# Moving the products dt times x of units 2 to 15 from GpSimd to VectorE in a one-core language-model tower

## The reference, cut to what matters

```python
def step(h, inp):
    u_t, dt_t, B_t, C_t = inp
    dA = jnp.exp(dt_t[..., None] * A)
    h = h * dA + (dt_t * u_t)[..., None] * B_t[:, None, :]
    y = jnp.einsum('bdn,bn->bd', h, C_t)
    return (h, y)
...
dt = jax.nn.softplus(x_dbl[..., :R] @ dt_w.T + dt_b)
```

## Time and profile before

| | |
|---|---|
| median of three runs | 551.28 us |
| the profiled execution | 551.16 us |
| its span in the trace | 549.3 us, 5677 instructions |
| VectorE (DVE) busy | 483.8 us, 88% |
| GpSimd (POOL) busy | 478.5 us, 87% |
| TensorE (PE) busy | 465.3 us, 85% |
| ScalarE (ACT) busy | 373.3 us, 68% |

### The profile page before, as it was taken

One profiled execution on the slowest core, in us unless ns is written; L12 is line 12 of the kernel. 1 busy time (PEld: TensorE's weight loads), 2 busy tenths in 40 slices (PEclk: granted clock), 3 DMA queues, 4 the chain that ended last, 5 costly groups with the idle time before them and its releaser, 6 DMA issues.

```text
span 549.3 us, 5677 instructions
## 1 busy us (share of the span) xinstructions
PE 465.3 (85%) x1659; PEld 181.0 (33%) x1659; DVE 483.8 (88%) x602; ACT 373.3 (68%) x656; POOL 478.5 (87%) x153
## 2 busy tenths in 40 slices
PE   6896886979799797979898889888997887795987
PEld 2432322323233232424233424343333332332333
DVE  3679879779898999999999999998899999999951
ACT  2475877476867777786968687858776885374633
POOL 5773889978979989899999999999999999999810
PEclk9897999889979898989999989979899998796999
DMA  5468641765071724426172717181717171700000
GB/s 60 27 48 236 209 155 40 249 217 157 32 242 38 234 78 150 162 93 218 62 231 83 239 63 248 54 253 54 252 50 253 58 253 48 256 16 10 0 11 19
DMA packets 50256, 70.79 MB, mean 129 GB/s; under 512 B 15874, under 2 KB 16818, under 8 KB 50226
## 3 DMA queue, kind: packets, MB, share of 16 engines
q1 hardware_dynamic: 47954, 69.20, 38.5%
q0 software_dynamic: 1024, 1.05, 3.3%
q10 hardware_dynamic: 1248, 0.19, 0.2%
HBM read 58.36 MB, written 9.96 MB: 124 GB/s over the span
## 4 chain that ended last, share of the span: by engine, by line
PE 36%; DVE 32%; issue 15%; ACT 8%; POOL 8%; DMA 0%; DVEq 0%; ACTq 0%; POOLq 0%
DVE st L1600 16%; DVE st L1585 6%; PE ps L638 6%; POOL st L506 5%; PE ps L731 3%; PE ps L719 3%; POOL st L497 2%; ACT ps L1114 2%; PE ps L813 2%; PE ps L549 2%; PE ps L699 2%; PE ps L681 2%; PE ps L829 2%; PE ps L612 2%; PE ps L665 2%
## 5 line engine op out<-in xcount | busy, mean ns | idle before, releaser
L506 POOL TENSOR_TENSOR st<-st,repC 128x2048 f32<-128x2048 f32 x63 | 285.9, 4547 | 21.0 <-ACT carry L1120 13.6
L1600 DVE TENSOR_TENSOR_SCAN st<-ps,carry,st 128x512 f32<-128x512 f32 x192 | 235.2, 1267 | 10.9 <-ACT ps L1114 10.3
L1114 ACT ACTIVATE ps<-dtS,negA 128x512 f32<-128x512 f32 x256 | 170.9, 682 | 47.2 <-DVE st L1600 43.9
L497 POOL TENSOR_TENSOR st<-duS,repB 128x2048 f32<-128x2048 f32 x31 | 141.0, 4548 | 2.0 <-PE ps L719 2.0
L1600 DVE TENSOR_TENSOR_SCAN st<-ps,zero,st 128x512 f32<-128x512 f32 x64 | 78.9, 1269 | 5.8 <-ACT ps L1114 5.4
L719 PE MATMUL ps<-st,fold 128*32 128x512 f32 x504 | 70.4, 625 | 15.4 <-POOL st L506 15.4
L1585 DVE TENSOR_TENSOR st<-duS,ps 128x2048 f32<-128x2048 f32 x32 | 72.7, 2271 | 0.2 <-PE ps L699 0.2
L638 PE MATMUL ps<-act,wT 128*128 128x512 f32 x128 | 57.7, 593 | 0.0
L470 POOL DMA_INDIRECT x<-in_L_tok_ple_table,idx x32 | 31.2, 976 | 12.5 <-issue 9.1
L681 PE MATMUL ps<-xr,wT 128*32 128x512 f32 x32 | 19.6, 697 | 22.5 <-DVE st L1585 22.5
L813 PE MATMUL ps<-xfT,w 97*128 97x512 f32 x64 | 35.2, 642 | 1.3 <-ACT xfT L1139 0.7
(11 more groups left out here) (150 smaller groups left out, 633.1 us busy)
## 6 DMA issues: line engine op xcount, KB each, us to landing
repC<-bc_dram SPq DMA_DIRECT2D x64, 256.0 KB, 4.8
duS<-du_dram SPq DMA_DIRECT2D x60, 256.0 KB, 3.3
dtS<-dt_dram SPq DMA_DIRECT2D x60, 256.0 KB, 4.2
repB<-bc_dram SPq DMA_DIRECT2D x31, 256.0 KB, 3.0
dt_dram<-dt SPq DMA_DIRECT2D x15, 256.0 KB, 3.2
du_dram<-du SPq DMA_DIRECT2D x15, 256.0 KB, 2.0
bc_dram<-bc_sb SPq DMA_DIRECT2D x16, 64.0 KB, 4.7
dtS<-dt SPq DMA_DIRECT2D x4, 256.0 KB, 5.7
```

The lines of the kernel that those rows point to most:

```text
L497: pool.tensor_tensor(st[:, r], duS[:, u % 2], row, ALU.mult).then_inc(sem("dbu_pool"), 1)
L506: pool.tensor_tensor(st[:, r], st[:, r], row, ALU.mult).then_inc(sem("hc_ready"), 1)
L1114: sc.activation(decay_bank(u, r, q), dtS[:, u % 2, q], ACT.Exp, scale=negA[:, way(u), q, r:r + 1]).then_inc(sem("decay_ready"), 1)
L1600: dve.tensor_tensor_scan(st[:, r, q, order], decay_bank(u, r, q)[:, order], st[:, r, q, order], first, ALU.mult, ALU.add).then_inc(sem("sc ...
```

## The change

For units 2 to 15, VectorE multiplies dt by x, and takes dt from the PSUM bank `PRE`, where TensorE has summed it, and not from ScalarE's copy. It still waits for `dt_ready`, that is, for the copy to be done. In units 2 to 13 the product for unit u+2 stands in slot 8 of VectorE; in unit 1 the product for unit 2 stands in slot 3 and that for unit 3 in slot 12. GpSimd keeps the product of unit 1 alone (unit 0's was VectorE's already).

Since the bank `PRE` is read until the product is done, what overwrites it waits for `du_ready` too: `conv` in that bank, and `pre`. ScalarE's `dt_out` no longer waits for `du_ready`, except for unit 2 (the copy `dt` is no longer an input of the product).

```diff
@@ gpsimd @@
-            def dt_times_x(u):
-                pool.wait_ge(sem("dt_ready"), u + 1)
-                if u == 1:
-                    for q in range(NQ):
-                        pool.wait_ge(sem(f"du_first_{q}"), 16)
-                else:
-                    pool.wait_ge(sem("du_in_dram"), 16 * (u - 1))
-                pool.wait_ge(sem("x_ready"), u + 1)
-                pool.tensor_tensor(du[:], dt[:], x_of(u), ALU.mult).then_inc(sem("du_ready"), 1)
+            def second_du():
+                pool.wait_ge(sem("dt_ready"), 2)
+                for q in range(NQ):
+                    pool.wait_ge(sem(f"du_first_{q}"), 16)
+                pool.wait_ge(sem("x_ready"), 2)
+                pool.tensor_tensor(du[:], dt[:], x_of(1), ALU.mult).then_inc(sem("du_ready"), 1)
...
                 if u == 0:
-                    dt_times_x(1)
+                    second_du()
                 if 2 in on_pool(u):
                     input_product(u, 2)
-                if u == 1:
-                    dt_times_x(2)
                 by_c(u, 0)
                 by_c(u, 1)
                 if u + 1 < UNITS:
                     input_product(u + 1, 0)
                 by_c(u, 2)
-                if 0 < u < UNITS - 2:
-                    dt_times_x(u + 2)
@@ tensor @@
                 if bank == PRE:
                     pe.wait_ge(sem("dt_ready"), u)
+                    pe.wait_ge(sem("du_ready"), u)
...
             def pre(u):
                 pe.wait_ge(sem("x_ready"), u + 1)
                 wait(pe, "dt_ready", u)
+                wait(pe, "du_ready", u)
...
                     if k == 0 and u == QUICK[0]:
-                        pe.wait_ge(sem("dt_ready"), UNITS)
+                        pe.wait_ge(sem("du_ready"), UNITS)
@@ scalar @@
-                sc.wait_ge(sem("du_ready"), u)
+                if u == 2:
+                    sc.wait_ge(sem("du_ready"), 2)
                 sc.activation(dt[:], ps[:, PRE, :], ACT.Copy).then_inc(sem("dt_ready"), 1)
@@ vector @@
+            def dt_times_x(u):
+                dve.wait_ge(sem("dt_ready"), u + 1)
+                dve.wait_ge(sem("du_in_dram"), 16 * (u - 1))
+                dve.wait_ge(sem("x_ready"), u + 1)
+                dve.tensor_tensor(du[:], ps[:, PRE, :], x_of(u), ALU.mult).then_inc(sem("du_ready"), 1)
...
+                if p == 3:
+                    if u == 1:
+                        dt_times_x(2)
...
+                if p == 8:
+                    if u != 1 and u + 2 < UNITS:
+                        dt_times_x(u + 2)
...
+                if p == 12:
+                    if u == 1:
+                        dt_times_x(3)
```

## The result

The changed kernel takes 566.06 us, the median of four runs (565.92 to 567.45), against 551.25 us for the kernel before beside it: 1.026 times as long, 95% interval 1.0218 to 1.0302. That is 14.8 us more (12.0 to 16.6 by the interval), where the prediction said 12.8 to 13; it is slower by more than 2%. In the experiments, a run more than 1.5% above the fastest of its kernel counts as slow and is left out of ratios and medians (one run of x2, three of x6, one of x8; with them the medians are 563.28, 549.18 and 553.53 us).

What follows compares the result with a forecast made beforehand. VectorE and GpSimd were taken as in balance in full units, with unit 1 bound by waits among VectorE, ScalarE and TensorE. 3.1 + 4.4 + 1.7 + 3.8 = 13.0 us over 551.16 gave 564 us; range 554 to 570 (8 in 10).

Steps and rivals of the forecast that it cites:

- The first wait: Unit 1: TensorE's pre(3) waits for unit 2's product behind scan 3, delaying decays from scan 4 on: +3.1 us.
- One sign: Unit 1, trace after: TensorE waits about 3 us before line 659's matmul, released by the product on VectorE.
- The lower bound of the clock's term: Unit 1: -1.9 us, if the low stretch at the pair at 96.28 (2.08 us) moves away.
- The second wait: Unit 1: unit 4's convolution in PRE waits for unit 3's product in slot 12; unit 2 starts 4.4 us later.
- The clock: TensorE in unit 1: low clock after the 4.4 us wait, +1.7 us, between -1.9 and +3.4.
- The three terms: Unit 1: first new wait 3.1 us, second new wait 4.4, TensorE's clock 1.7.
- Units 2 to 13: VectorE pays 0.6 us in 8 units, 4.8 us; GpSimd's relief gives back about 1.0: +3.8 us, bounds -0.7 and +7.2.
- A: From unit 6 on GpSimd sets the pace; nine products leave, 11.1 us, giving 540 us; chance 0.05.
- B: Unit 1's shift is given back in units 2 to 5; only VectorE's added time counts: 555 to 559.6 us; chance 0.25.
- C: Slot 8: VectorE stalls for ScalarE's late copy; half of 12 units lose 1 us, 570 us; chance 0.08.

Runs made afterwards that it cites:

- x2: Kernel before, with only the products of units 2 and 3 on VectorE from PSUM, in slots 3 and 12 of unit 1: 561.33 us, ratio 1.0165.
- x6: Kernel before, with GpSimd's products of units 4 to 15 made over 1 of 512 columns and nothing added to VectorE: 546.97 us, ratio 0.9938.
- x8: Kernel before, with only the products of units 9, 11 and 13 on VectorE from PSUM: 553.38 us, ratio 1.0048.
- x1: The change, with the products of units 2 and 3 back on GpSimd: 554.84 us, ratio 1.0042 to the kernel before.
- x3: Kernel before, with only the product of unit 2 on VectorE from PSUM, slot 3 of unit 1: 554.42 us, ratio 1.0042.
- x10: Kernel before, with only the product of unit 3 on VectorE from PSUM, slot 12 of unit 1: 561.84 us, ratio 1.0158.
- x9: The change, with seven zero-adding matmuls on TensorE ahead of unit 1's waiting convolution: 563.28 us, ratio 1.0201 to the kernel before.
- x7: The change, with each of VectorE's 14 products made twice in a row: 574.78 us, ratio 1.0448 to the kernel before.

## Why the prediction was right, step by step

**The first wait** was put at 3.1 us. Scan 4 came 3.4 us late, by the path that was forecast. One sign came out smaller: TensorE waited 1.67 us for the product, and not about 3. Ahead of `pre(3)` in its queue the sum of dt for unit 2 ran at the low clock (2.08 and 1.79 us for its first two pairs, from 81.85; 1.12 and 1.02 before), so that TensorE came to `pre(3)` 1.7 us later in the unit anyhow. That stretch needs no product: x1, where the products of units 2 and 3 are GpSimd's, has one there too, and its scan 4 comes 1.7 us late, behind this wait (0.58 before):

```profile
90.95 1.28 DVE L1612 TENSOR_TENSOR_SCAN st<-ps,carry,st 128x512 f32<-128x512 f32 x1 [2.27 <-ACT ps L1126]
```

In x3 that sum runs at the full clock: TensorE waits 3.34 us, and scan 4 comes 4.0 us late, 0.6 of it because the pair of `pre(3)` then takes 1.69 us (grant 0.64 from 90 to 92). I had taken the clock to stay full behind this wait. What I had not followed either is that the stretches of low clock change their place within the unit. In the change the matmuls of y times z at 95.75 took 2.08 us in place of 1.12, and VectorE waited 0.98 us for them; in return the sum of dt for unit 3, which ran at the low clock before (2.08 us at 96.28), ran at the full one (1.12 at 101.56), and VectorE's wait before scan 11 shrank from 2.57 to 0.88 us. The lower bound of the clock's term named that last stretch as one that could move away. Alone this wait cost 2.3 us (0.3 to 4.3; x3).

**The second wait** was put at 4.4 us and the trace shows 4.43, in x10 as well. **The clock** was put at 1.7 us; the convolution took 5.77 us in place of 3.60, 2.2 more, and x9 shows that the wait is its cause. The three terms made 9.2 us, and unit 1 is 9.4 us longer: 2.8 by which TensorE was late at the convolution, 4.43 and 2.2.

**Units 2 to 13** were put at 3.8 us. From the start of unit 2 to that of unit 14 it is 353.82 us now and was 349.79: 4.0. That this is so near is luck. In x3 and x10 all twelve products made there are GpSimd's, as before, and the same stretch takes 353.13 and 352.71 us, 3.3 and 2.9 more than before; in x1, with all twelve moved, it takes 349.94, 0.2 more. So one trace doesn't resolve this term. By its ratio x1 puts it at 2.3 (0.2 to 4.5), which the 3.8 fits. Its parts were only roughly right: I had 4.8 us paid in 8 units, 4 units hiding theirs, and 1.0 given back. x7 (0.62 for each further product) and units 7 and 8 above speak for the full price in more units, and x6 for a relief of 3.4, not 1.0; 12 x 0.6 less 3.4 gives 3.8 too, but that this is how the time is made up is argued and not shown.

**The rivals.** A wanted VectorE to have 1.8 us free per unit; x6 gives GpSimd the relief for nothing and gains 3.4 us, not 11. B wanted the shift of unit 1 to be taken back; x2 keeps 9.1 us of it, at least 4.5. C does not appear. That the median is 2 us above the forecast I cannot split: the four runs agree on 566 to 567.5, while those of x1 and x2 spread over 7 and 9 us. In the profiled execution, 16.3 us longer than that before, 1.0 us lies ahead of unit 1, where no product was moved. A further 2.1 us come from the tail, where six matmuls of one expert layer run at the low clock:

```profile
545.17 4.96 PE L808 MATMUL ps<-xfT,w 97*128 97x512 f32 x6 [0.67 <-ACT xfT L1135]
```

They took 2.84 us before.

## What to carry to other kernels

An operation that reads a PSUM bank in place of its copy keeps the bank shut until its slot comes up in its engine's queue, so cost the move by the wait of the bank's next writer, and not by the operation alone: 12 products of 0.6 us cost 2.3 us here (0.2 to 4.5), and two cost 9.1 (4.5 to 13.7). The slot decides: place such a reader directly behind the point where its input is ready, best where the engine waits anyhow. When two engines are in balance, leaving work out on one of them (x6) tells at once what moving it can gain at most. And compare a stretch of one trace with the same stretch of other kernels that have the same code there, before a small difference is put down to the change.

## What the runs showed of the hardware that I had not expected

In 13 of 14 cases a VectorE product with both inputs in SBUF lasted until the GpSimd instruction that was running had ended (up to 4.38 us for work of 0.67), and with one input in PSUM it lasted 661 to 667 ns in all 14 cases beside the same GpSimd work. Reading dt from PSUM, which shut the bank, is also what kept this change from costing 47 us.
